# The sum behind the channel norm, moved from VectorE to GpSimd

## What is computed

```
x = _layernorm(x + _L0_attn_ref(x, q_w, k_w, v_w, o_w))        # 16 heads, causal, ALiBi
x = _layernorm(x + _L0_ffn_ref(x, w_freq_real, w_freq_imag, bias))
x = _layernorm(x + _L1_attn_ref(x, w_qkv, b_qkv, w_fc, b_fc, gamma, beta))
x = _layernorm(x + _L1_ffn_ref(x, centroids, ln_g, ln_b, w1, b1, w2, b2))
```

```
out = out @ w_fc + b_fc
out = out + x
mu = mean(out); var = mean((out - mu) ** 2)
out = (out - mu) * rsqrt(var + EPS) * gamma + beta
```

## Time and profile before

| | before |
|---|---|
| median of three runs | 1402.78 us (1401.7 to 1404.92) |
| profiled execution, time | 1403.28 us |
| profiled execution, span | 1401.5 us |
| PE busy | 1339.0 us, 96% |
| DVE busy | 1067.6 us, 76% |
| ACT busy | 837.7 us, 60% |
| POOL busy | 262.8 us, 19% |

### The profile page before, as it was taken

One profiled execution on the slowest core, in us unless ns is written; L12 is line 12 of the kernel. 1 busy time (PEld: TensorE's weight loads), 2 busy tenths in 40 slices (PEclk: granted clock), 3 DMA queues, 4 the chain that ended last, 5 costly groups with the idle time before them and its releaser, 6 DMA issues. The chain is left out here.

```text
span 1401.5 us, 43928 instructions
## 1 busy us (share of the span) xinstructions
PE 1339.0 (96%) x18306; PEld 814.0 (58%) x18306; DVE 1067.6 (76%) x1991; ACT 837.7 (60%) x1767; POOL 262.8 (19%) x440
## 2 busy tenths in 40 slices
PE   7999899999999999999999999999987699999998
PEld 4554344434444444444444444587765589999997
DVE  2566998989899899899898992467567677666765
ACT  3455668778788688686886886533345433343332
POOL 4332112102112121121021111100125511111111
PEclk9999999999999999999999999999999899999999
DMA  7696511212111212212210000313615654455441
GB/s 224 201 205 132 92 26 33 49 32 48 41 41 41 47 35 46 43 39 47 69 48 4 3 3 2 119 31 132 221 49 178 208 202 180 179 184 185 175 165 75
DMA packets 78208, 134.34 MB, mean 96 GB/s; under 512 B 12354, under 2 KB 64827, under 8 KB 72636
## 3 DMA queue, kind: packets, MB, share of 16 engines
q1 hardware_dynamic: 59996, 109.11, 27.0%
q10 hardware_dynamic: 14608, 14.00, 3.2%
q0 software_dynamic: 3408, 8.43, 1.7%
HBM read 68.01 MB, written 23.11 MB: 65 GB/s over the span
## 5 line engine op out<-in xcount | busy, mean ns | idle before, releaser
L1948 DVE TENSOR_REDUCE part_max<-pair 128x2 f32<-128x1024 f32 (+2 forms) x576 | 641.6, 1158 | 64.2 <-PE pair L1320 33.0
L1732 ACT ACTIVATE big<-pair 128x512 f32<-128x512 f32 (+1 forms) x1120 | 580.2, 609 | 151.4 <-PE pair L1348 142.7
L1348 PE MATMUL pair<-big 128*32 128x512 bf16 (+3 forms) x5120 | 346.1, 349 | 5.2 <-DMA big<-max_t 2.0
L1320 PE MATMUL pair<-big 128*32 128x512 bf16 (+3 forms) x5120 | 341.4, 348 | 9.6 <-DVE part_max L1948 9.4
L1370 PE MATMUL pair<-big 128*17 128x512 f32 (+3 forms) x2560 | 288.7, 529 | 0.9 <-POOL big L2431 0.8
L1320 PEld LDWEIGHTS pair<-big 128*32 128x32 bf16 x5120 | 128.1, 96 | 185.6 <-DVE part_max L1948 90.0
L1348 PEld LDWEIGHTS pair<-big 128*32 128x32 bf16 x5120 | 125.8, 96 | 183.9 <-ACT big L1732 112.2
L1745 ACT ACTIVATE std<-moments,eps_col 128x1 f32<-128x1 f32 (+1 forms) x102 | 30.1, 295 | 238.6 <-DVE moments L1991 238.6
L1623 PE MATMUL pair<-big,tok 128*128 128x128 f32 x1248 | 147.6, 277 | 5.3 <-DVE big L2307 5.3
L1623 PEld LDWEIGHTS pair<-big,tok 128*128 128x128 f32 x1248 | 146.6, 194 | 8.6 <-DVE big L2307 6.7
L1635 PE MATMUL pair<-big 128*128 x624 | 141.0, 379 | 0.0
(11 more groups left out here) (213 smaller groups left out, 1226.1 us busy)
## 6 DMA issues: line engine op xcount, KB each, us to landing
tok<-big SPq DMA_DIRECT2D x39, 1024.0 KB, 4.7
big<-in_L_ffn_w SPq DMA_DIRECT2D x16, 1024.0 KB, 14.3
big<-split_dram SPq DMA_DIRECT2D x216, 64.0 KB, 2.7
split_dram<-big ACTq DMA_DIRECT2D x32, 384.0 KB, 4.0
big<-split_dram SPq DMA_DIRECT2D x42, 256.0 KB, 4.3
big<-routed_dram SPq DMA_DIRECT2D x39, 129.0 KB, 2.1
tok<-in_L_attn_x SPq DMA_DIRECT2D x8, 512.0 KB, 7.0
big<-in_c_query_rows SPq DMA_DIRECT2D x8, 512.0 KB, 4.7
```

The costliest lines, as they stand in the source:

```text
L1320: mm = pe.matmul(bank[q:q + STRIPE, o:o + w], m.q_op[slot][:, step.qt, h, step.r * P + q:step.r * P + q + STRIPE], m.k_op[slot][:, h, step ...
L1348: mm = pe.matmul(m.bank[step.bank][k:k + STRIPE, n * w:(n + 1) * w], m.k_op[slot][:, h, step.kb * P + k:step.kb * P + k + STRIPE], m.q_op[ ...
L1732: act.activation(m.p_ring[:, step.place, step.heads[0]:step.heads[-1] + 1, step.at:step.at + w], m.bank[step.bank][:, 0:len(step.heads) * ...
L1948: dve.tensor_reduce(m.part_max[(step.u * QT + step.qt) % 2][:, step.r, step.heads[0]:step.heads[0] + n, step.c], banks[:, :, 0:w], X, ALU. ...
```

## The change

The step Combine goes from VectorE's list to GpSimd's. In the plan its cost becomes 2750 ns on "pool" (it was 1300 ns on "dve"), and its choices stand behind those of ShiftBeta. In the code one instruction over four blocks (128 x 1024) becomes four over one block each (128 x 256), each behind a wait for that block's beta, and the last of them gives the semaphore `combined`.

```
-                yield ready, 0, self.run, ("dve", Combine(g), self.COMBINE, ready, ("second", g))
+                yield ready, 0, self.run, ("pool", Combine(g), 2750, ready, ("second", g))
...
                                 ("dve", (self.add_choices(), self.norm_choices(), self.shift_choices(),
-                                         self.combine_choices(), self.soon_choices())), ("pool", (self.beta_choices(),))):
+                                         self.soon_choices())),
+                                ("pool", (self.beta_choices(), self.combine_choices()))):
...
-        elif isinstance(step, Combine):
-            g = step.g
-            dve.wait_ge(s.added, 2 * plan.multiply_of["C", g] + 2)
-            dve.wait_ge(s.beta_added, BPT * (g + 1))
-            dve.tensor_tensor(m.group(g), m.group(g), m.res[g % 2][:, :, :], ALU.add).then_inc(s.combined, 1)
...
+        elif isinstance(step, Combine):
+            pool.wait_ge(s.added, 2 * plan.multiply_of["C", step.g] + 2)
+            for r in range(BPT):
+                row = m.group(step.g)[:, r, :]
+                pool.wait_ge(s.beta_added, BPT * step.g + r + 1)
+                done = pool.tensor_tensor(row, row, m.res[step.g % 2][:, r, :], ALU.add)
+            done.then_inc(s.combined, 1)
```

## The result

The changed kernel is slower: 1408.43 us in the median of 10 runs against 1403.09 us for the kernel before beside it, a ratio of 1.0033, 95% interval 1.0018 to 1.0047. The profiled execution has a span of 1406.8 us, 5.3 us longer than before. The forecast was 1407.6 us, slower.

What follows compares the result with a forecast made beforehand. It took a chain of waits through several engines (Scale, Combine, Moments, Roots, Squares, Scale) as the bound. 1.3 + 3.9 - 1.1 + 0.35 + 0.4 = +4.85 us on 1402.78 gave 1407.6 us, 8-in-10 range 1402.8 to 1411.5.

Steps and rivals of the forecast that it cites:

- Tiles 0 to 3 and the folding: Up to tile 4: HeadSoftmax late behind Moments 2, so FoldChannel waits for ScalarE's half; +1.3 us, bounds 0 and +1.65.
- GpSimd's queue at tile 4: Combine 4 waits behind the scatters of tile 1, holding up Moments 4 and Scale 5; +3.9 us, bounds -0.3 and +3.9.
- The cycles behind it: Scale 5 to Scale 7: cycles of 6.6 us instead of 7.2; -1.1 us for two, bounds -1.5 to +2.
- Best 2: Behind Scale 7: Shift 6 now precedes Best 2, +0.35 us; Combine 7 beside Best 2 and Choose 2 slows VectorE, +0.4.
- Rival E: Best 2 and Choose 2 get through only when Combine 7 is done: 2.6 instead of +0.4, 1409.8 us; chance 0.06.
- Rival A: Combine 4 gets on GpSimd ahead of tile 1's scatters: tile-4 term -0.5, time 1403.2 us, no change; chance 0.18.
- Rival B: Outer norm leaves the cycle, Moments behind the next tile's Scale on VectorE: 5.2 us cycles, 1398.5 us; chance 0.09.
- Rival C: Second halves of tiles 6 and 7 on PE run at the slow clock and bind: some +2, 1409.6 us; chance 0.09.

Runs made afterwards that it cites:

- e5: Changed kernel with HeadSoftmax of batch 1 ahead of Moments 2 on VectorE, its exponentials ahead of that tile's Roots on ScalarE: 1417.84 us, ratio 1.0036.
- e2: Changed kernel with the scatters of tile 1 moved behind Combine 7 in GpSimd's list: 1402.53 us, ratio 0.9997 to the kernel before.
- e7: Changed kernel with Combine on GpSimd as one instruction over 128 x 1024 instead of four: 1418.16 us, ratio 1.0032 to the kernel before.
- e6: Changed kernel with Combine 7 alone back on VectorE, between PlaceRows 2 and Moments 7: 1416.65 us, ratio 1.0027 to the kernel before.
- e1: Changed kernel with Combine 4 moved ahead of the scatters of tile 1 in GpSimd's list: 1408.1 us, ratio 1.0044 to the kernel before.
- e4: Changed kernel's order, but VectorE makes Combine in one instruction right ahead of its tile's Moments: 1398.3 us, ratio 0.9966 to the kernel before.
- e3: Kernel before with its order kept, but Combine on GpSimd right behind its tile's beta: 1411.43 us, ratio 1.0066 to the kernel before.
- e10: Changed kernel, unchanged, run again as a control on another chip: 1415.15 us, ratio 1.0017 to the kernel before.

## Why the prediction was right

The steps that it named appear where it said: the scatters of tile 1 ahead of Combine 4, Moments 4 ahead of Scale 5, Squares ahead of Roots, and HeadSoftmax late behind Moments 2. Against the sum, term by term, from the table and the traces of before and changed:

- *Tiles 0 to 3 and the folding*: +1.3 forecast, +1.0 measured at Scale 4. The wait ahead of FoldChannel ended with ScalarE, as said, and e5 removes it by moving the step that was named.
- *GpSimd's queue at tile 4*: +3.9 forecast, +3.4 measured (Scale 5 62.93 against 58.54 us after Scale 0, less the 1.0). Combine 4 began at 1060.17 and not at 1060.75, since its tile was 1.0 late and not 1.3, and the second of the four scatters took 0.96 us where it had taken 1.30 before. e2 shows it: with the scatters out of the way Scale 5 follows Scale 4 after 6.56 us, not 10.51.
- *The cycles behind it*: -1.1 forecast, -1.2 measured (13.25 us for two against 14.45). The two were to be 6.6 us each and took 6.95 and 6.30, the first with 0.55 us of waiting for the slow half of tile 6.
- *Best 2*: +0.35 and +0.4 forecast, +0.83 (from Scale 7 to Best 2) and +0.93 (from there to PlaceRows 3) measured. This is the term that was mis-sized, 1.76 us for 0.75.
- The sum was +4.85; it is +4.95 at PlaceRows 3 and +4.9 at the fetch. The overestimate of the queue and the underestimate of Best 2 cancelled: that the sum is right to 0.1 us is partly luck. The timed runs differ by 5.3 us (1408.43 against 1403.09), 0.4 more than the traces do at the fetch; as much is found behind it, 304.6 against 304.25 us.

What was wrong in the last term is the reading of one row. The prediction took from Shift's 0.43 us that an instruction of VectorE on two SBUF operands waits 0.26 us for GpSimd. It had started at 1065.80 us, in the middle of one of the adds of beta 6:

```profile
1064.19 2.61 POOL L2454 TENSOR_TENSOR tok<-tok,big 128x256 f32<-128x256 f32 x4 [2.15 <-PE pair L1437]
```

Four adds in 2.61 us, each 0.68 long, start about 0.64 apart, so the third ran from about 1065.5 to 1066.15 (an estimate from this row and the earlier trace rows), and Shift ended at 1066.23. In the changed kernel Shift 6 starts at 1079.73 with the first add of Combine 7 (1079.69) and takes 0.70 us, and in e7 it takes 2.17 us beside one instruction of 2.18: it waits to the end of the GpSimd add that is running. The excess of Shift 6 and of three instructions of Best 2 is 0.54 + 0.29 + 0.38 + 0.15 = 1.36 us, where +0.4 was forecast with 1.3 as the upper bound, and e6, where none of them has a neighbour, gets 1.37 back by Count 2. The rest of the 1.76 is Shift 6 itself, for which +0.35 was forecast, and about 0.1 behind Count 2. The Trainium skill ("SBUF — State Buffer", section "SBUF: two separate sides") describes an exclusive lock, held for a whole instruction by whoever starts first, and these traces agree, within 0.03 us in e7. Rival E had the mechanism, and was wrong only in holding Best 2 until all of Combine 7 was done: its instructions end at 1081.03, 1081.74 and 1082.33 us, inside the stretch of Combine 7 or just behind it, so between two adds VectorE gets a turn.

Rival A was priced wrongly. It gave all of the queue's cost back for putting Combine 4 ahead of the scatters; e1 did just that and got 0.2 us in these cycles. The scatters of tile 1 hold GpSimd for 5.1 us, and as long as they stand between two Combines the later of the two waits for them; only behind the last one (e2) are they out of the way. Rival B's idea, the norm out of the loop, is what the planner had done by half, with Squares ahead of Roots and Scale ahead of Shift, and e4 shows what that is worth when VectorE makes the sum. Rival C's slow half of tile 6 came about (3.38 us) and was hidden as the forecast said but for 0.55 us ahead of Scale 6; tile 7's half ran at the full clock again, in 1.89 us. One slip in the working has no weight: 1033.32 + 1.65 is 1034.97, not 1034.95.

So two things changed at once, with opposite signs. With VectorE making the sum, the new order is worth -4.1 us (e4). With the old order, GpSimd making the sum costs +9.1 us (e3); there Combine 4 is ahead of the scatters and Combine 5 waits for them, which shows in the starts of Scale, 8.55, 10.10 and 8.55 us apart. They add up to +5.0, where the changed kernel has +5.3.

## What to carry to other kernels

An in-order engine that looks 80% idle is not free for a step on the critical path: ask what stands ahead of that step in its queue, and whether moving it ahead only lets the next one be late (e1) or takes the blocker out of the loop (e2). Where a planner makes the order, a changed cost is two changes, the step's price and a new order; run each alone, since here the better half could be kept without the other and beat both kernels. A short VectorE instruction on two SBUF operands beside GpSimd arithmetic cost up to a whole GpSimd instruction here (2.17 us in e7), so a long single instruction on GpSimd can lose as much as it saves when such neighbours are on the path.

## What the runs showed of the hardware

FoldChannel's 16 matrix multiplications took 3.72, 5.4 or 6.76 us. It goes with the granted clock: 1.00 over those of e1 and e3, 0.68 over those of the changed kernel, 0.55 over those of e2. In the stretch from 1034 to 1040 us it was 0.72 before and 1.00 in e4, here in this order:

```profile
1034.00:1040.00 6.00, 5.41 (x18) 4.47 (x19) 3.10 (x14) 0.60 (x3) 0.00 (x0) 0.72 0.00 0
```

```profile
1034.00:1040.00 6.00, 5.24 (x25) 4.54 (x25) 4.97 (x20) 1.18 (x4) 0.36 (x2) 1.00 0.00 0
```

PE had waited 1.92 us ahead of it before and 1.64 us in e4. It repeats on another chip: 5.38 in both traces of the kernel before, 3.72 in both of the kernel of e4. But with the same wait of 2.03 or 2.04 us ahead, at the same distance from Scale 0, they ran for 5.41 (changed, e6, e10), 3.72 (e1, e3) and 6.76 us (e2). What decides between them these traces don't show; it is worth 1.7 to 3 us. In e4's trace, 5.9 us ahead of the kernel before at the fetch, 1.7 are this, 0.3 FoldChannel's earlier start, and 4.1 the cycles from Scale 4 to Scale 7 (less 0.2 behind them). Whether the 1.7 recur in most executions is not shown; the medians differ by 4.1 us (1398.3 against 1402.36).

Two other chips needed 10 us more for the same kernel in the median. The two traces of the kernel before differ by 7.7 us: 2.8 of these lie between PlaceRows 3 and the first fetch and 3.9 behind it (308.2 against 304.25 us), with waits that the profile puts down to nothing. An effect of 1 us can only be seen in the traces there, counted from a common step.
